# Attention in a fused block: the band masks move from TensorE to VectorE's reduction, key 0 and query 0 move into the bands

## The chip, the cores and the metric

One Trainium2 chip; the kernel runs on one of its NeuronCores. The metric is device time in microseconds (us), the median of several runs. The data path is float32 throughout. Where a product must be exact to float32, both operands are split into a high part (float32r) and a low part, and three products are summed.

## The reference

The program is one transformer layer over x of shape 8 x 512 x 256: layer norm, attention with a mask, residual, layer norm, a mixture of experts, residual. The changed part is the attention:

```python
Q, K, V = (split_heads(xn @ W + b) for W, b in ((Wq, bq), (Wk, bk), (Wv, bv)))    # 16 heads of 16
window_ok = abs(i - j) <= 64
global_ok = (i == 0) | (j == 0)              # query 0 sees all keys, all queries see key 0
scores = einsum('bhqd,bhkd->bhqk', Q, K) * 0.25 + where(window_ok | global_ok, 0, -inf)
out = einsum('bhqk,bhkd->bhqd', softmax(scores), V)
```

After it, each of 16 experts takes its 512 best tokens, computes (gelu(x Wg) * (x Wu)) Wd and adds the weighted rows to the output; 1024 inner columns, 256 outer ones. A shared expert runs for all tokens.

## The kernel before

The program has four blocks, one after another, with a barrier between them: `project` (layer norm, q, k and v), `attend`, `front` (output projection, norm, gate, shared expert, choice of tokens) and `experts`. Each engine has its own stream of instructions in a fixed order written by hand; they meet only at semaphores.

`project` works batch by batch. TensorE makes q and k (four tiles of 128 rows x 512 tokens); ScalarE writes the high parts (line 248), VectorE the low parts (line 299); SP writes all four to the scratch tensor `qk_parts` with one DMA a batch (line 201) from one of two buffers. GpSimd only clears buffers and casts the mask.

`attend` works in steps. One step is one batch and four heads (HQ = 4), so there are 8 x 4 = 32 steps. For each of a step's heads, the keys and queries are cut into four tiles of 128. Tile 0 holds the global key and the global query and is computed against all 512 columns; each other tile only against its window of 256 or 192 columns.

- Scores (`score_job`, lines 633 to 653). Queries on the partitions. They serve only to find each query's maximum. TensorE first writes the mask into PSUM as a bfloat16 product with the identity (line 646), adds the product q k (line 648), and, for tiles 1 to 3, makes a product with keys 0 and 1 alone (line 651). VectorE reduces a group of two or four heads at a time (line 550), the far columns of query 0 apart (line 552), and takes in key 0 (line 555).
- The negated maximum, split in two parts (lines 559 and 561), is transposed by VectorE (line 567) and carried by four small DMAs (`m_rows`, line 495) into rows 96 and 97 of `qs`. There it joins the contraction, so that the second product comes out with the maximum already subtracted.
- Exponents (`st_job`, lines 655 to 675). Keys on the partitions. TensorE makes k q minus the maximum (lines 668 and 670; only tile 0 has a mask product, line 667), and a product with queries 0 and 1 for tiles 1 to 3 (line 673). ScalarE takes the exponential into `pt` (line 610), and that of query 0 into `pq` (line 602). GpSimd zeroes what lies outside the window with two affine selections a tile (line 454).
- Value products (`times_v`, lines 677 to 702), in plain float32, four heads side by side on the array: the window (line 691), the rest of key 0's row (line 697), query 0's column (line 700). One extra column of ones gives the denominators. ScalarE empties the bank (line 595), SP stores it (line 499).

TensorE's order in step u (`body`, line 705) is: for g from 0 to 4, the scores of group g of step u + 2, two exponent jobs of step u, and, from g = 1 on, the value products of tile g - 1 of step u - 1. Scores have two PSUM buffers (of two banks), exponents two of one bank. The loops over batches are hardware loops with the first and last batch peeled.

SP's queue in step u: the four DMAs of `m_rows(u + 1)`; then it waits until TensorE has finished the exponent products of step u and issues the six loads of step u + 4 (line 485), each of 16 partitions x 4 heads x 512 tokens; then the store of step u - 1. Once a batch it also fetches the denominators (`load_den`) and, at t = 3, writes their reciprocals back and waits until they have landed (`store_rden`, line 509 and the wait behind it). VectorE makes those reciprocals after the maxima of step u + 1.

`experts` runs 16 experts. TensorE makes 8 row tiles of h (line 1913); VectorE, ScalarE and GpSimd turn them into high and low parts, GpSimd's low part being the last (line 1803). Then come four output tiles of 128 tokens, each 8 chunks x 3 products (line 1931), in two alternating PSUM banks, which ScalarE empties (line 1849). Output tile 0 waits chunk by chunk for the low parts.

Of the kernel before, what the change touches and what calls it, by code (L numbers as in the profile page):

```python
# [29 lines left out]
P = 128  # L30
# [20 lines left out]
M_ROW = 96  # L51

# [4 lines left out]
W = [h - l for l, h in zip(LO, HI)]  # L57

# [18 lines left out]
def build(nc, d):  # L77

    with ExitStack() as ctx:
# [6 lines left out]
        d["qk"] = scratch("qk_parts", (B, 4, D, S))  # L86
# [12 lines left out]
        ks = att.enter_context(nc.sbuf_tensor("ks", [P, UB, HQ, S], F32R))  # L99
        qs = att.enter_context(nc.sbuf_tensor("qs", [P, UB, HQ, S], F32R))  # L100
        v = att.enter_context(nc.sbuf_tensor("v", [P, B * NT, D], F32))

        mask = att.enter_context(nc.sbuf_tensor("mask16", [P, S + 2 * P], BF16))
# [32 lines left out]
def project(nc, d, sem, tally, ident, bias, eps, ks, qs, vs, mask, ident16):  # L136
    with ExitStack() as ctx:
# [15 lines left out]
        qk = sb("qk", [P, 2, 4, KD, S], F32R)  # L153
        m32 = sb("mask32", [P, S + 2 * P])
# [21 lines left out]
        qlo_s = sem("p_qlo")  # L176
        v_s = sem("p_v")
# [3 lines left out]
        with nc.Block() as block:  # L181
            @block.sync
            def _(sp):
# [45 lines left out]

            @block.scalar  # L230
            def _(act):
# [10 lines left out]
                def qk_hi(b, h, first):  # L242
                    for n in range(4):
# [4 lines left out]
                        act.activation(qk[:, h, 2 * w, m], ps_qk[:, n], ACT.Identity,  # L248
# [23 lines left out]
            def _(dve):  # L272
# [22 lines left out]
                def qk_lo(b, h):  # L295
                    for n in range(4):
                        w, m = n // 2, n % 2
                        dve.wait_ge(qhi_s, b * 4 + (n + 1))
                        dve.scalar_tensor_tensor(out=qk[:, h, 2 * w + 1, m], in0=ps_qk[:, n],
                                                 scalar=bias[:, w, m:m + 1], in1=qk[:, h, 2 * w, m].bitcast(F32),  # L300
# [88 lines left out]
def attend(nc, d, sem, tally, ks, qs, vs, mask, ident16):  # L389
    with ExitStack() as ctx:  # L390
# [3 lines left out]
        SL = UB  # L394
        vx = sb("vx", [P, 2, NT, HQ * VW])
        mx = sb("mx", [P, 2, HQ, NT])
        far = sb("far", [1, HQ])
        nm = sb("nm", [P, 2, HQ * NT], F32R)
        mt = sb("mt", [P, 2, 32])
        pt = [sb(f"pt{i}", [P, 2, HQ, W[i]]) for i in range(NT)]  # L400
        pq = sb("pq", [P, 2, HQ, NT - 1])
# [3 lines left out]
        ps_s = ctx.enter_context(nc.psum_tensor("ps_s", [P, 2, 2 * S], F32))  # L405
        ps_p = ctx.enter_context(nc.psum_tensor("ps_p", [P, 2, S], F32))

        ps_x = ctx.enter_context(nc.psum_tensor("ps_x", [P, 2, HQ, NT - 1, 2], F32))
        key0, query0 = ps_x[:, 0], ps_x[:, 1]  # L410
        ps_o = ctx.enter_context(nc.psum_tensor("ps_o", [P, S], F32))
        qk_in = [sem(f"a_qk_in{s}") for s in range(SL)]
        ones_s = sem("a_ones")
        v_s = sem("a_v")
        m_in = [sem(f"a_m_in{s}") for s in range(SL)]
        sc_s = sem("a_sc")
        mx_s = sem("a_mx")
        mk_s = sem("a_mk")
# [4 lines left out]
        q0_s = sem("a_q0")  # L423
        av_s = sem("a_av")
        sel_s = sem("a_sel")
        nrm_s = sem("a_nrm")
# [6 lines left out]
        GROUPS = [(0, h, 2) for h in range(0, HQ, 2)] + [(j, 0, HQ) for j in range(1, NT)]  # L433
        TJOBS = [(0, h, 1) for h in range(HQ)] + [(i, h, 2) for i in range(1, NT) for h in range(0, HQ, 2)]
        GJ, SJ = len(GROUPS), len(TJOBS)
        EOF = [sum(j[0] < i for j in TJOBS) for i in range(NT + 1)]
        N0 = P + WIN
        MK = P // 32

        def after(b, t, n):

            return b + (t + n) // UB, (t + n) % UB

        with nc.Block() as block:
            @block.gpsimd
            def _(pool):
                def window(b, t, i):

                    wait_alone(pool, tally, exp_s, b * (UB * SJ) + (t * SJ + EOF[i + 1]))
                    for lo, hi, sign in ((0, P, 1), (P, W[i], -1)):
                        part = pt[i][:, t % 2, :, lo:hi]
                        last = pool.affine_select(out=part, in_=part, pattern=[[0, HQ], [sign, hi - lo]],  # L454
                                                  compare_op=ALU.is_ge, fill=0.0, base=0, channel_multiplier=-sign)
                    last.then_inc(sel_s, 1)

                def take_v(b, t, fresh):
                    if not fresh:
                        wait_alone(pool, tally, av_s, b * UB + (t - 1))  # L460
                    src = vs[:, bass.ds(b * NT, NT), t * HQ * DH:(t + 1) * HQ * DH].rearrange("p n (h c) -> p n h c", c=DH)
                    dst = vx[:, t % 2].rearrange("p n (h c) -> p n h c", c=VW)[:, :, :, 0:DH]
                    pool.tensor_copy(dst, src).then_inc(v_s, 1)
# [3 lines left out]
                for t in range(UB):  # L467
                    take_v(0, t, t < 2)
                    for i in range(1, NT):
                        window(0, t, i)  # L470
                with pool.Fori(1, B) as b:
                    for t in range(UB):
                        take_v(b, t, False)
                        for i in range(1, NT):
                            window(b, t, i)

            @block.sync
            def _(sp):
                def load(b, t):

                    def heads(part):
                        return d["qk"][b, part, t * HQ * DH:(t + 1) * HQ * DH, :].rearrange("(h c) q -> c h q", c=DH)

                    for row, part, dst in QK_ROWS:
                        sp.dma_start(dst[row:row + DH, t].bitcast(F32), heads(part)).then_inc(qk_in[t], 16)
# [1515 lines left out]
```

## Time and profile before

| | us |
|---|---|
| median of 3 runs | 1401.46 (1398.49 to 1401.52) |
| the profiled execution | 1400.23 |
| its span | 1398.5 |
| TensorE matmul busy | 1256.7 (90%) |
| VectorE busy | 849.4 (61%) |
| ScalarE busy | 597.1 (43%) |
| GpSimd busy | 584.9 (42%) |
| `attend`: first score, last value product | 119.7, 515.8 |
| `experts`: one expert, start to start | 36.3 |

The span runs from the first to the last recorded instruction; the execution's own time is 1.7 us longer. The page's granted TensorE clock is 0.9 or more in most of its 40 slices, among them all slices of the expert block from 840 us on, and lower where one block hands over to the next. In a timeline, one row can stand for several like instructions (x8); the duration of a matmul is that from its start to its modelled end, and consecutive matmuls overlap, so what a matmul costs is read from start to start, which the prediction calls its pitch. The same holds for VectorE, where a following instruction starts before the end of the one ahead.

### The profile page before, as it was taken

How to read it: one execution, taken by the hardware profiler on the slowest of the kernel's cores; microseconds unless marked ns; L12 is line 12 of the kernel's file. 1: busy time of each engine (PE TensorE's matmuls, PEld its weight loads, DVE VectorE, ACT ScalarE, POOL GpSimd, SP SyncE). 2: the span in 40 equal slices, each digit the busy share in tenths (PEclk: the TensorE clock that was granted, in tenths of full speed). 3: DMA queues.
4: the chain of work that ended last, by engine and by line, in shares of the span. 5: the costliest groups of instructions: out<-in, count | busy, mean ns of one | idle time of the engine just before them, and what ended most of it. 6: DMA issues, size and time to landing. Idle time of an engine off the chain costs nothing. (4 is left out here: it accounts for less than half of the span.)

```text
span 1398.5 us, 26404 instructions
## 1 busy us (share of the span) xinstructions
PE 1256.7 (90%) x9930; PEld 1066.7 (76%) x9930; DVE 849.4 (61%) x1510; ACT 597.1 (43%) x1023; POOL 584.9 (42%) x530
## 2 busy tenths in 40 slices
PE   2995999999999972699999599999999999999997
PEld 2884777777777752588887578888888888888886
DVE  7874555555555512695688676666666666666641
ACT  1340544444444442354222255455455454545442
POOL 6000333332333342462200146666666666665554
PEclk9996999999999985699999789999999999999999
DMA  2778555555555416441003144434444433344411
GB/s 84 262 249 136 79 88 90 86 86 92 93 93 93 71 50 198 144 149 57 15 31 121 51 161 121 115 105 113 120 121 121 121 111 105 109 114 121 121 31 15
DMA packets 71284, 148.44 MB, mean 106 GB/s; under 512 B 14736, under 2 KB 31520, under 8 KB 64928
## 3 DMA queue, kind: packets, MB, share of 16 engines
q1 hardware_dynamic: 58544, 128.39, 35.4%
q0 software_dynamic: 12656, 18.90, 7.4%
q8 instruction: 56, 0.92, 0.3%
q14 instruction: 28, 0.23, 0.1%
HBM read 104.53 MB, written 42.21 MB: 105 GB/s over the span
## 5 line engine op out<-in xcount | busy, mean ns | idle before, releaser
L610 ACT ACTIVATE pt<-ps_p 128x512 f32<-128x512 f32 (+1 forms) x320 | 170.0, 582 | 218.1 <-PE ps_x L673 122.7
L550 DVE TENSOR_REDUCE mx<-ps_s 128x2 f32<-128x384 f32 (+2 forms) x160 | 143.9, 900 | 171.9 <-PE ps_x L651 154.9
L1803 POOL TENSOR_TENSOR h_lo<-h,h_hi 128x512 fp32r<-128x512 f32 x128 | 175.5, 1383 | 136.1 <-ACT h_hi L1839 135.8
L454 POOL TENSOR_SCALAR_AFFINE_SELECT pt<-pt 128x512 f32<-128x512 f32 x192 | 110.1, 597 | 273.4 <-ACT pt L610 273.4
L1913 PE MATMUL ps_gu<-xt_hi,w_hi 128*128 128x512 f32 x512 | 203.5, 397 | 2.1 <-DVE xt_lo L1862 2.1
L1913 PE MATMUL ps_gu<-xt_lo,w_hi 128*128 128x512 f32 x512 | 200.8, 392 | 0.0
L1913 PE MATMUL ps_gu<-xt_hi,w_lo 128*128 128x512 f32 x512 | 200.3, 391 | 0.0
L1878 DVE TENSOR_TENSOR h<-ge,ps_gu 128x512 f32<-128x512 f32 x128 | 87.8, 686 | 180.1 <-ACT ge L1833 167.9
L1740 DVE TENSOR_TENSOR w_lo<-w,w_hi 128x768 fp32r<-128x768 f32 x128 | 173.5, 1360 | 31.3 <-ACT w_hi L1735 27.8
L648 PE MATMUL ps_s<-ks,qs 96*128 96x256 f32 (+2 forms) x512 | 171.6, 398 | 0.0
L1812 POOL DMA_INDIRECT out<-ys,idx x64 | 131.1, 2049 | 73.3 <-ACT ys L1849 61.8
L1931 PE MATMUL ps_y<-w_hi,h_hi 128*128 128x256 f32 x512 | 146.4, 286 | 14.6 <-POOL h_lo L1803 14.6
L646 PE MATMUL ps_s<-mask,ident 128*128 128x256 bf16 (+1 forms) x512 | 139.4, 276 | 16.9 <-DMA ks<-qk_parts 15.9
L1931 PE MATMUL ps_y<-w_lo,h_hi 128*128 128x256 f32 x512 | 144.8, 283 | 0.0
L1931 PE MATMUL ps_y<-w_hi,h_lo 128*128 128x256 f32 x512 | 144.7, 283 | 0.0
L1833 ACT ACTIVATE ge<-ps_gu 128x512 f32<-128x512 f32 x128 | 76.2, 596 | 123.1 <-PE ps_gu L1913 122.4
L1707 POOL DMA_INDIRECT xg<-h_rows,idx x64 | 63.5, 992 | 126.8 <-DVE idx L1698 107.0
L1735 ACT ACTIVATE w_hi<-w 128x768 fp32r<-128x768 f32 x128 | 106.4, 837 | 16.7 <-PEq L880 16.7
L1913 PEld LDWEIGHTS ps_gu<-xt_hi,w_hi 128*128 128x128 f32 x512 | 96.9, 189 | 21.5 <-issue 2.5
L1913 PEld LDWEIGHTS ps_gu<-xt_hi,w_lo 128*128 128x128 f32 x512 | 96.8, 189 | 20.6
L1931 PEld LDWEIGHTS ps_y<-w_hi,h_hi 128*128 128x128 f32 x512 | 98.0, 191 | 18.5 <-POOL h_lo L1803 17.8
L1913 PEld LDWEIGHTS ps_gu<-xt_lo,w_hi 128*128 128x128 f32 x512 | 97.0, 189 | 18.6
(221 smaller groups left out, 2891.9 us busy)
## 6 DMA issues: line engine op xcount, KB each, us to landing
w<-in_We SPq DMA_DIRECT2D x48, 1024.0 KB, 4.9
qk_parts<-qk SPq DMA_DIRECT2D x8, 2048.0 KB, 7.7
qs<-qk_parts SPq DMA_DIRECT2D x96, 128.0 KB, 3.6
ks<-qk_parts SPq DMA_DIRECT2D x96, 128.0 KB, 5.0
x<-in_x SPq DMA_DIRECT2D x16, 512.0 KB, 8.7
attn_t<-on SPq DMA_DIRECT2D x32, 256.0 KB, 3.7
ot<-attn_t SPq DMA_DIRECT2D x32, 128.0 KB
rd<-rden SPq DMA_DIRECT2D x16, 256.0 KB
```

What stands on the lines that cost most here:

```text
L454: last = pool.affine_select(out=part, in_=part, pattern=[[0, HQ], [sign, hi - lo]], compare_op=ALU.is_ge, fill=0.0, base=0, channel_multip ...
L550: last = dve.tensor_reduce(mxu[:, h:h + n, j], tile[:, :, 0:N0 if j == 0 else W[j]], AX, ALU.max)
L610: act.activation(pt[i][:, t % 2, h:h + nh], ps_p[:, n % 2].rearrange("p (h q) -> p h q", h=nh)[:, :, 0:W[i]], ACT.Exp, scale=SCALE).then_i ...
L646: pe.matmul(tile[:, 0:masked], ident16[:], mask[:, m_off:m_off + masked], start=True, stop=False, skip_group_check=True)
L648: last = pe.matmul(tile[:, 0:W[j]], q, ks[0:M_ROW, t, h, LO[j]:HI[j]], start=False, stop=True, skip_group_check=True)
L1735: act.activation(self.hi[:, s, cs], self.w32[:, cs], ACT.Copy).then_inc(self.hi_s, 1)
L1740: eng.tensor_tensor(self.lo[:, s, cs], self.w32[:, cs], self.hi[:, s, cs].bitcast(F32), ALU.subtract).then_inc(self.lo_s, 1)
L1803: pool.tensor_tensor(h_lo[:, m], h32[:, (e * KI + m) % HB], h_hi[:, m].bitcast(F32), ALU.subtract).then_inc(hlo_s, 1)
L1812: pool.indirect_dma_start(d["out"], bass.IndirectOffsetOnAxis(ap=idx[:, e % SLOTS, c:c + 1], axis=0), ys[:, e % 2, c], None, compute_op=AL ...
L1878: dve.tensor_tensor(h32[:, (e * KI + m) % HB], ge[:, m % 2], ps_gu[:, m % 2, 1], ALU.mult).then_inc(h_s, 1)
L1913: last = pe.matmul(ps_gu[:, m % 2, n], l, r, start=c == 0, stop=c == 3 * KD - 1)
L1931: last = pe.matmul(ps_y[:, t % 2, 0:D], l, r, start=c == 0, stop=c == 3 * KI - 1)
```

## The change

Layout. In `qk_parts`, `ks` and `qs` each tile of 128 tokens gets a 129th column (ZC = 129), which holds a copy of token 0: key 0 in `ks`, query 0 in `qs`. A window that starts or passes there therefore contains the global key or query, and is two columns wider (WZ = 258, 258, 194). GpSimd writes the copies in `project`, after the low parts and before the write. The rows of Wq and Wk are permuted on the way in, so that one load reads one run of 4 x 516 floats for each of its 16 partitions.

```diff
-                    sp.wait_ge(qlo_s, b * 4 + 4)
-                    sp.dma_start(d["qk"][b].rearrange("c (m p) q -> p c m q", p=P),
-                                 qk[:, h].bitcast(F32)).then_inc(out_s[h], 16)
+                    sp.wait_ge(z_s, b + 1)
+                    sp.dma_start(d["qk"][b].rearrange("c (m t) d h q -> (t d h) c m q", m=KD),
+                                 qk[:, h].rearrange("p c m k i -> p c m (k i)").bitcast(F32)).then_inc(out_s[h], 16)
...
+                for b in range(B):
+                    pool.wait_ge(qlo_s, b * 4 + 4)
+                    rows = qk[:, b % 2].rearrange("p c m k i -> p (c m) k i")
+                    pool.tensor_copy(rows[:, :, :, P], rows[:, :, 0, 0:1].to_broadcast([P, 4 * KD, NT])).then_inc(z_s, 1)
```

Scores. One product a head and tile, without a mask, in a ring of three banks. VectorE adds the mask (bfloat16, in SBUF) and takes the maximum in one instruction, 16 a step.

```diff
+                    if n >= RING:
+                        pe.wait_ge(mx_s, n + 1 - RING)
+                    q = tile_of(qs[0:M_ROW, t, h], j)
+                    k = ks[0:M_ROW, t, h]
+                    k = whole(k) if j == 0 else window(k, j)
+                    out = ps_s[:, n % RING]
+                    out = out.rearrange("p (k c) -> p k c", c=P) if j == 0 else out[:, 0:WZ[j]]
+                    pe.matmul(out, q, k, start=True, stop=True).then_inc(sc_s, 1)
...
+                        n, m = (S, mask[:, 0:S]) if j == 0 else (WZ[j], mask[:, S:S + WZ[j]])
+                        dve.tensor_tensor_reduce(junk[:, (u * SG + g) % RING, 0:n], ps_s[:, (u * SG + g) % RING, 0:n], m, 1.0, -3e38, ALU.add, ALU.max,
+                                                 mx[:, u % 2, h, j:j + 1]).then_inc(mx_s, 1)
```

Exponents. Two heads a job throughout, in two buffers of two banks; the product with query 0 alone and `pq` go, since query 0 is a column of the band (`FAR`). Before the products of a step ScalarE copies the two maximum rows of query 0 to the added columns (`far_rows`), and TensorE waits for that. GpSimd masks pieces of 64 columns (`near_only`: 4, 4 and 3 selections a step in place of two a tile).

TensorE's order. Each of eight places of a step has two scores of step u + 2 and one exponent job of step u; the value products of step u - 1 stand at two places.

```diff
+                for u in range(NU):
+                    for n in range(SJ):
+                        if u + 2 < NU:
+                            score(u + 2, 2 * n)
+                            score(u + 2, 2 * n + 1)
+                        exponents(u, n)
+                        if u >= 1 and n in (5, 7):
+                            times_v(u - 1, n - 5)
+                            times_v(u - 1, n - 4)
```

SP's queue and the reciprocals. The loops of `attend` are unrolled on all engines.

```diff
+                for u in range(NU):
+                    b, t = u // UB, u % UB
+                    if u + 1 < NU:
+                        m_rows(u + 1)
+                    if 1 <= u <= NU - UB:
+                        sp.wait_ge(st_s, u * SJ)
+                        load(u + UB - 1)
+                    if u >= 2:
+                        store(u - 2)
+                    if b >= 1 and t == 2:
                         load_den(b - 1)
+                    if b >= 1 and t == 3:
                         store_rden(b - 1)
...
+                for u in range(NU):
+                    maxima(u)
+                    if u >= 9 and u % UB == 1:
+                        reciprocals((u - 9) // UB)
                 reciprocals(B - 2)
```

Experts. Chunks 0 to 6 of output tiles 0 and 1 go ahead of chunk 7 of both:

```diff
+                    if e > 0:
+                        pe.wait_ge(ys_s, e * CT)
+                    contract(0, range(KI - 1))
+                    contract(1, range(KI - 1))
+                    contract(0, range(KI - 1, KI)).then_inc(y_s, 1)
+                    contract(1, range(KI - 1, KI)).then_inc(y_s, 1)
+                    for t in range(2, CT):
+                        pe.wait_ge(ys_s, e * CT + (t - 1))
+                        contract(t, range(KI)).then_inc(y_s, 1)
```

## Rows read from the trace of the kernel before

**Rows 1.** Windows, one step: engines' busy us (instructions), granted clock, DMA share, GB/s.
```profile
core 0: us, PE busy (x) PEld busy (x) DVE busy (x) ACT busy (x) POOL busy (x), PEclk, DMA share, GB/s
253.10:265.20 12.10, 12.07 (x142) 9.38 (x142) 6.66 (x12) 5.73 (x13) 3.83 (x8) 1.00 0.52 91
```
**Rows 2.** Timeline of TensorE in a step: start us, duration us, engine, line, operation.
```profile
250.18 0.28 PE L646 MATMUL ps_s<-mask,ident 128*128 128x256 bf16 x1
...
250.46 0.36 PE L670 MATMUL ps_p<-qs,ks 128*128 128x256 f32 x1
...
251.44 0.64 PE L691 MATMUL ps_o<-pt,vx 128*32 128x256 f32 x8
...
252.04 0.36 PE L670 MATMUL ps_p<-qs,ks 128*128 128x192 f32 x1
...
254.59 0.26 PE L646 MATMUL ps_s<-mask,ident 128*128 128x192 bf16 x1
...
254.94 0.26 PE L646 MATMUL ps_s<-mask,ident 128*128 128x192 bf16 x1
...
257.66 0.53 PE L691 MATMUL ps_o<-pt,vx 128*32 128x192 f32 x8
...
258.80 0.28 PE L646 MATMUL ps_s<-mask,ident 128*128 128x256 bf16 x1
```
**Rows 3.** Timeline of an expert's contraction; in brackets idle time and releaser.
```profile
1018.70 0.28 PE L1931 MATMUL ps_y<-w_hi,h_lo 128*128 128x256 f32 x1
...
1019.89 0.39 PE L1931 MATMUL ps_y<-w_hi,h_hi 128*128 128x256 f32 x1 [0.91 <-POOL h_lo L1803]
...
1020.55 0.47 ACT L1849 ACTIVATE ys<-ps_y,wt 128x256 f32<-128x256 f32 x1 [0.35 <-PE ps_y L1931]
```
**Rows 4.** Timeline of TensorE, products of 512 and 256 columns without a mask.
```profile
683.99 0.39 PE L1456 MATMUL ps_gu<-ht_b,sw_lo 128*128 128x512 f32 x1
684.22 0.28 PE L1491 MATMUL ps_y<-sw_hi,h_hi 128*128 128x256 f32 x1
684.34 0.28 PE L1491 MATMUL ps_y<-sw_lo,h_hi 128*128 128x256 f32 x1
```
**Rows 5.** Timeline of VectorE, an operation with an accumulator.
```profile
684.65 0.75 DVE L1205 TENSOR_SCALAR_CACHE_REDUCE junk<-seg_probs,cand 128x512 bf16<-128x512 f32 x1
685.32 0.08 DVE L1205 DVE_READ_ACCUMULATOR junk<-seg_probs,cand 128x1 f32 x1
685.32 0.68 DVE L1158 TENSOR_TENSOR h<-ge,ps_gu 128x512 f32<-128x512 f32 x1
```
**Rows 6.** Timeline of VectorE, a scan and a plain two-input operation.
```profile
760.52 1.23 DVE L1242 TENSOR_TENSOR_SCAN run<-equal,zero 128x512 f32<-128x512 f32 x1
...
789.91 0.42 DVE L1168 TENSOR_TENSOR x<-ps_y,x 128x256 f32<-128x256 f32 x1
790.25 1.21 DVE L1682 TENSOR_TENSOR hot<-pm,iota 128x1024 bf16<-128x1024 bf16 x1
```
**Rows 7.** Timeline of VectorE, the end of a step's maxima.
```profile
255.46 0.17 DVE L559 TENSOR_SCALAR nm<-mx 128x16 fp32r<-128x16 f32 x1
...
256.07 0.56 DVE L550 TENSOR_REDUCE mx<-ps_s 128x2 f32<-128x384 f32 x1
```
**Rows 8.** Timeline of SP's queue: loads, the reciprocals' write, maximum rows.
```profile
277.60 1.30 SPq L485 DMA_DIRECT2D qs<-qk_parts  x3
...
282.69 0.36 SPq L509 DMA_DIRECT2D rden<-den  x1
286.51 2.62 SPq L495 DMA_DIRECT2D qs<-mt  x4
```
**Rows 9.** One line, 277 to 281 us: duration ns min/median/max, first and last start.
```profile
L485 SPq DMA_DIRECT2D ks<-qk_parts x3: 316/316/369, 279.1 to 280.0; - x3
...
DMA to landing us min/median/max: 3.0/4.4/5.4
```
**Rows 10.** Windows: the last write of q and k; the queued first loads.
```profile
106.00:109.00 3.00, 0.00 (x0) 0.00 (x0) 0.00 (x0) 0.00 (x0) 0.00 (x0) 0.80 1.05 367
122.00:125.00 3.00, 2.96 (x17) 2.46 (x16) 2.13 (x4) 0.00 (x0) 0.00 (x0) 0.50 1.09 131
```

More of the change, by code:

```diff
@@ L51 @@
 M_ROW = 96
+RING = 3
+ZC = P + 1
+ZS = NT * ZC
 LO = [0] + [P * i - WIN for i in range(1, NT)]
@@ L430, in attend, with whole, window, tile_of @@
         rden_out = sem("a_rden_out")
[L433 to L436, printed above, removed]
+        SCORES = [(j, h) for j in range(NT) for h in range(HQ)]
+        TJOBS = [(i, p) for i in range(NT) for p in range(HQ // 2)]
+        SG, SJ = len(SCORES), len(TJOBS)
         N0 = P + WIN
         MK = P // 32
-        def after(b, t, n):
-            return b + (t + n) // UB, (t + n) % UB
+        LOADS, MROWS = 6, MK
+        def whole(tile):
+            return tile.rearrange("p (k c) -> p k c", c=ZC)[:, :, 0:P]
+        def window(tile, n):
+            return tile[:, ZC * n - WIN - 1:ZC * n - WIN - 1 + WZ[n]]
+        def tile_of(tile, n):
+            return tile[:, ZC * n:ZC * n + P]
         with nc.Block() as block:
@@ L466, in _ @@
                 pool.wait_ge(ones_s, 1)
-                for t in range(UB):
-                    take_v(0, t, t < 2)
+                for u in range(NU):
+                    take_v(u)
                     for i in range(1, NT):
[L470 to L475, printed above, removed]
+                        near_only(u, i)
@@ L477, in _ @@
             @block.sync
             def _(sp):
[L479 to L485, printed above, removed]
-                QK_ROWS = [(DH * r, part, dst) for dst, parts in ((qs, (0, 0, 1)), (ks, (2, 3, 2)))
-                           for r, part in enumerate(parts)]
@@ L655, in st_job @@
[L655 to L665 removed]
+                        pe.wait_ge(qk_in[t], (b + 1) * 16 * LOADS)
@@ L675, in st_job, with near @@
                     last.then_inc(st_s, 1)
-                def times_v(b, t, i, first):
+                def near(rows, v, p, i):
+                    out = ps_o[rows, LO[i]:HI[i]]
+                    if i < NT - 1:
+                        pe.matmul(out.rearrange("p (k c) -> p k c", c=WIN), v,
+                                  p.rearrange("p (k c) -> p k c", c=WIN + 1)[:, :, 0:WIN],
+                                  start=False, stop=True, skip_group_check=True)
+                    else:
+                        pe.matmul(out[:, 0:WIN], v, p[:, 0:WIN], start=False, stop=True, skip_group_check=True)
+                        pe.matmul(out[:, WIN:W[i]], v, p[:, WIN + 1:W[i] + 1], start=False, stop=True, skip_group_check=True)
@@ L693, in times_v @@
                     for h in range(HQ):
-                        rows = slice(32 * h, 32 * h + 32)
-                        v = vx[:, t % 2, i, h * VW:(h + 1) * VW]
+                        rows, v = slice(32 * h, 32 * h + 32), vx[:, s, i, h * VW:(h + 1) * VW]
                         if i == 0:
-                            last = pe.matmul(ps_o[rows, N0:S], v[0:1], pt[0][0:1, t % 2, h, N0:S], start=False, stop=True,
+                            last = pe.matmul(ps_o[rows, N0:S], v[0:1], pt[0][0:1, s, h, N0:S], start=False, stop=True,
@@ L698, in times_v @@
                                              skip_group_check=True)
                         else:
-                            last = pe.matmul(ps_o[rows, 0:1], v, pq[:, t % 2, h, i - 1:i], start=False, stop=True,
+                            z = FAR[i]
+                            last = pe.matmul(ps_o[rows, 0:1], v, pt[i][:, s, h, z:z + 1], start=False, stop=True,
                                              skip_group_check=True)
```

354 lines of the change are left out of this document (149 added, 205 removed).

## The prediction

> **What bounds the kernel now.** I read the windows of single attention steps first, because the change touches the attention block, one wait of the projection block and one loop of the expert block. A step (one batch, four of 16 heads; 32 in all) takes 12.1 us; TensorE is busy for 12.07 of them at granted clock 1.00, VectorE for 6.66, ScalarE for 5.73, GpSimd for 3.83 [rows 1]. TensorE never stops, the others stand for half of the time, so its stream is the step. Then I took its timeline apart by start to start [rows 2]: a mask, a windowed score and a two-column key-0 product are 250.18 to 250.46, 0.28 us for one head; a mask and a 512-column product 0.35 us (254.59 to 254.94); the value products of a 256-wide key tile 0.60 us (251.44 to 252.04), those of tile 0 1.14 us (257.66 to 258.80). The expert block I read by its one regular hole: each expert's TensorE stops before the last contraction chunk, 1018.70 to 1019.89 [rows 3], against a pitch of 0.12 us (684.22 to 684.34) [rows 4], so for 1.07 us.
>
> **TensorE's step afterwards.** Masks and two-column products leave the scores: 4 of 512 columns, 8 of 258, 4 of 194. A 512-column float32r product alone has pitch 0.23 us (683.99 to 684.22), a 256-column one 0.12 [rows 4]; 258 I put at 0.125, and 194 at 0.12 too (bounds 0.08, in proportion to its columns, and 0.12: a window of 192 in the present step is no cheaper than one of 256). Scores: 0.92 + 1.0 + 0.48 = 2.4 us. Exponent products: 4 x 0.35 for tile 0 with its mask, 12 x 0.12 without their partners = 2.8. Value products keep their work; the 64-wide pieces split one matmul of tile 3 in two (4 more a step) and the query-0 column is read from the band: 1.14 + 0.60 + 0.60 + 0.55 = 2.9. The sum is 8.1 us instead of 12.1. If TensorE stayed the bound that would be 4 us x 32 = 128 us. It does not.
>
> **VectorE's step afterwards.** Instead of 5 reductions, 2 far reductions and 2 small maxima it runs 16 add-and-maximum instructions, 4 over 512 elements, 8 over 258, 4 over 194, each with an accumulator. The trace has none. Nearest rows: a 512-element operation with accumulator goes from 684.65 to the next full instruction at 685.32, 0.67 us, the accumulator read (0.08) lying beside its successor [rows 5]; a plain two-input operation of 256 has pitch 0.34 (789.91 to 790.25) [rows 6]. I take 0.67, 0.40 and 0.34: 2.68 + 3.2 + 1.35 = 7.2 us. Bounds: 0.61, 0.34, 0.27 (6.2 us in all), and the 1.23 us of the scan over 512, half the rate [rows 6], with 0.67 and 0.53 for the shorter ones (about 0.13 plus two cycles' share an element): 12.4 us. I take the accumulator row as the nearest kind. The tail (two small operations and the transpose) is 255.46 to 256.07, 0.61 us [rows 7], and about 0.25 for the last reduction's end: 0.85.
> The Trainium skill ("VectorE: DVE Perf Modes", Rules for kernel authors) says to minimise the number of VectorE operations, since each pays its drain; this speaks against 16 operations in place of 9. By the pitch rows each of the 16 carries about 0.13 us that no element pays for, and that is in my sum.
>
> **How the two interlock.** TensorE's scores run three banks ahead at most (RING = 3). After score 11 it makes one exponent job and the value products of tiles 0 and 1: 0.13 + 0.24 + 1.14 + 0.60 us, and 0.4 until score 12 can be read: 2.5 us, while VectorE holds at most three reductions less what has run, 1.1 us. It idles 1.4 us. After score 15 the hole is 2.0 us against 1.0 us of reductions and 0.85 of tail: idle 0.3 with the wake-ups. VectorE's cycle is 7.2 + 0.85 + 1.4 + 0.3 = 9.8 us; TensorE waits for it. ScalarE has the same exponentials in fewer instructions (5.7 us now), GpSimd 11 selections instead of 6, at most 0.6 us each by its 3.83 us for 7 instructions [rows 1], 7 us: both hide below 9.8. The copy of far rows takes the place of the query-0 exponentials.
>
> **SP's queue, which moves.** Per step it issues four row DMAs (286.51, 2.62 us), then six loads; the first is issued at 277.60 [rows 8] and the sixth at 280.0, landing 5.4 us later [rows 9], 7.8 us in all. The rows of step u+1 wait for its maxima, the loads stand behind them, and they bring what the scores of step u+3, run at the start of step u+1, need. Before, loads started 1.3 us before a step and had the whole 12.1 us. Now the chain is 2.6 + 0.4 + 7.8 = 10.8 us from the end of the maxima. Over two steps: scores and maxima of a step about 9.6 us (9.8 less their late start), then 10.8: 20.4, or 10.2 a step, hardly above VectorE's 9.8 and partly taken up; I take 10.1. The rows of a load are now one run of 8256 bytes instead of four of 2048. Bounds for the load burst: 4.9 us (issue and the earliest landing of 3.0) to 8.5; I take no gain: the queued loads at the start, 2048-byte runs into 16 partitions, move 131 GB/s at full DMA share, the write of q and k, also in 2048-byte runs but over 128 partitions, 367 [rows 10]. So the narrow target holds them, not the run length, and it stays.
> The Trainium skill ("SBUF — State Buffer", Door 1: The DMA port swizzle) states that 16 partitions reach only 4 of the 16 ports and measures 104 GB/s there. The trace agrees in kind, its 131 GB/s being for loads that overlap on two such ranges.
> **The wait inside the queue.** store_rden waits on SP until its DMA has landed: from 282.69 to the next issue at 286.51, 3.8 us [rows 8]. Before, the loads had slack. Now SP reaches it in step 4b+3, and the reciprocal (0.54 us) stands behind maxima(4b+5), the very maxima whose rows are queued next. Those rows, the loads and the scores behind them are 0.54 + 3.8 = 4.4 us late. It hits 6 times (u = 7 to 27; at 31 no load follows): 26 us.
> **Attention in sum:** 30 steps x (12.1 - 10.1) = 60, less 26 = 34 us. The first body is some 3 us shorter, the last two, without scores, about as much longer behind ScalarE and GpSimd: nought. The start is DMA and VectorE as now. Unrolled loops: priced at nothing (bounds -2 to +5), the expert block being straight code already.
>
> **Projection.** GpSimd's 32-element copy (about 0.4 us) goes between the last low part and the write of q and k. Batches hide it behind the other half's buffer; after the last batch the barrier feels it: +0.4 us (0 to 2, should rows of 2064 bytes write worse).
>
> **Experts.** Chunks 0 to 6 of tiles 0 and 1 now go before chunk 7: 21 more matmuls, 2.5 us, cover the 1.07. But tile 2 needs bank 0 emptied: 0.28 to the end of its last matmul, 0.05, 0.47 us for the copy (1020.55) [rows 3] and 0.05 to wake, against 0.36 us of chunk 7 of tile 1: a new stop of 0.45. Net 0.6 x 16 = 10 us (bounds 0 and 17).
>
> **Sum:** the profiled execution took 1400.2 us (span 1398.5), within 0.1% of the median 1401.46. 1400.2 - 34 - 10 + 0.4 = 1357 us.
>
> **Rivals.**
> (B) The load chain never binds: longer runs land sooner. For it: a quarter of the descriptors, and writes in the rows may be slower than reads for another reason than the target. Then 9.8 us a step and between none and half of the 26 us: 1400 - 69 - 10 = 1321, or 1337.
> (C) The new operation carries 0.1 us more overhead: 16 x 0.1, of which 1.3 a step shows: about 1395, little or no gain. For it: it is an operation that the trace doesn't have; against: the accumulator row.
> (D) Slower: the add-and-maximum runs at two cycles an element, like the scan [rows 6]. VectorE then needs 12.4 + 0.85 + about 1 = 14.2 us: 32 x 2.1 - 10 = 57 us more, 1458. It decides from 0.17 us above my price per instruction. 
> (E) The clock: TensorE, now waiting a fifth of each step and 4 us at six places, is granted 0.50. In the first stretch of attention it stood at 0.50 (1.2 GHz) although TensorE was busy for 2.96 of 3.00 us [rows 10]. At half the clock a step of 8.1 us comes to some 15: about 1490. Against: the expert block keeps 0.9 or more in every slice of the page in spite of its stops.
>
> **Chances:** forecast 0.42 (own range 1340 to 1377), B 0.20, C 0.20, D 0.10, E 0.08. 1322 to 1397 leaves out D, E and a little of B and C. What a measurement tells from no change is 0.3%, 4 us. Faster by more: 0.42 + 0.20 + 0.15 = 0.77; within: 0.05 of C; slower 0.18.
>
> **What would show it.** In the trace after: VectorE near 8 us busy in a step of 10, and TensorE near 80%, waiting for the maxima; pitches of 0.67, 0.40 and 0.34; one step in four near 14.5 us, with TensorE waiting for the DMA of ks and SP standing behind rden; in the experts a stop of 0.45 us in place of 1.07, behind the copy of ps_y. Steps under 9.6 us, or no long fourth step, would prove the queue argument wrong; pitches above 0.8 us my choice among the rows.

## The result, and the profile after

The changed kernel takes 1357.22 us (median of 4 runs, 1356.25 to 1364.43); the kernel before, beside it on the same chip, 1401.49 (4 runs, 1398.49 to 1406.84). The ratio is 0.969, 95% interval 0.965 to 0.974, and the prediction was 1357. The profiled execution took 1356.66 us, span 1354.9. What the spans lost, 1398.5 - 1354.9 = 43.6 us, I cut at three events of TensorE in both timelines: the last value product of attention starts at 515.8 before and 487.8 after (28.0 us less); from there to the first product of expert 0 it is 292.4 and 288.9 us (3.5 less, in code that the change doesn't touch); the experts follow from the line below.

Instructions of one line (TensorE, first product of the experts): duration ns min/median/max, first to last start. First the kernel before, then the one after.
```profile
L1913 PE MATMUL ps_gu<-xt_hi,w_hi x512: 389/389/767, 808.2 to 1376.8; 128*128 128x512 f32 x171
```
```profile
L1885 PE MATMUL ps_gu<-xt_hi,w_hi x512: 389/389/764, 776.7 to 1333.9; 128*128 128x512 f32 x171
```
568.6 against 557.2 us: 11.4 less, and 0.7 in the end that is left.

The step. These windows answer to [rows 1]: an undisturbed step, and the next, which waits for loads.
```profile
core 0: us, PE busy (x) PEld busy (x) DVE busy (x) ACT busy (x) POOL busy (x), PEclk, DMA share, GB/s
253.95:263.71 9.76, 9.71 (x109) 6.40 (x109) 7.25 (x36) 5.83 (x10) 3.35 (x9) 1.00 0.71 111
263.71:277.21 13.50, 9.76 (x118) 6.41 (x108) 7.50 (x36) 5.82 (x10) 5.60 (x16) 1.00 0.54 90
```
By the starts of the first score of each step, the 29 steps from 133.88 to 453.06 us are: 10.7 and 12.9 at the start (10.7 the first body, without value products), then 21 ordinary ones, mostly in a pattern of 10.6, 10.8 and 9.8 (mean 10.45), and a long one at u = 8, 12, 16, 20, 24 and 28: 12.5, 13.5, 12.4, 12.6, 12.7, 12.6. The places are the predicted ones; the lengths are not (10.1 and 14.5). In the first body TensorE makes two scores and then stands for ScalarE's copy of the far rows:
```profile
137.03 0.50 PE L637 MATMUL ps_p<-mask,ident 128*128 128x192 bf16 x2 [1.96 <-ACT qs L586]
```

VectorE's timeline, which answers to [rows 5] and [rows 6]: start us, duration us, operation.
```profile
250.83 0.36 DVE L548 CUSTOM_DVE_ANT_0 junk_s<-ps_s,mask 128x194 bf16<-128x194 f32 x1 [1.71 <-PE ps_s L625]
251.12 0.08 DVE L548 DVE_READ_ACCUMULATOR2_ANT mx<- 128x1 f32 x1
251.12 0.35 DVE L548 CUSTOM_DVE_ANT_0 junk_s<-ps_s,mask 128x194 bf16<-128x194 f32 x1
251.40 0.08 DVE L548 DVE_READ_ACCUMULATOR2_ANT mx<- 128x1 f32 x1
...
255.22 0.69 DVE L548 CUSTOM_DVE_ANT_0 junk_s<-ps_s,mask 128x512 bf16<-128x512 f32 x1
...
255.83 0.69 DVE L548 CUSTOM_DVE_ANT_0 junk_s<-ps_s,mask 128x512 bf16<-128x512 f32 x1
...
257.05 0.42 DVE L548 CUSTOM_DVE_ANT_0 junk_s<-ps_s,mask 128x258 bf16<-128x258 f32 x1
...
257.40 0.42 DVE L548 CUSTOM_DVE_ANT_0 junk_s<-ps_s,mask 128x258 bf16<-128x258 f32 x1
```
The pitches are 0.61 (255.22 to 255.83), 0.35 (257.05 to 257.40) and 0.28 us (251.12 to 251.40), and the accumulator read costs nothing of its own. They sum to 4 x 0.61 + 8 x 0.345 + 4 x 0.28 = 6.3 us.

SP's queue across a long step, answering to [rows 8], then what TensorE does at its end:
```profile
264.08 0.34 SPq L515 DMA_DIRECT2D rden<-den  x1
266.67 2.58 SPq L500 DMA_DIRECT2D qs<-mt  x4
269.31 1.32 SPq L492 DMA_DIRECT2D qs<-qk_parts  x3
270.67 1.58 SPq L492 DMA_DIRECT2D ks<-qk_parts  x3
```
```profile
277.21 0.73 PE L625 MATMUL ps_s<-ks,qs 96*128 96x512 f32 x2 [3.69 <-DMA ks<-qk_parts]
```
SP stands from 264.42 to 266.67 behind the write of the reciprocals, although the maxima of that step were transposed by 263.61 (VectorE's row at 263.40, 0.21 us). Rows and loads go out late, and TensorE stops for 3.69 us. This is the longest of the six: here the write lands 2.6 us after its issue, in four of the others after 1.5. The other five long steps have stops of 2.61 to 2.86 us, and the second step has one of 2.70.

Waits between 110 and 490 us (engine and line, what it waited for: us, times, longest):
```profile
PE ps_s L625 <- DMA ks<-qk_parts: 43.6, 17, 15.9
PEld ps_s L625 <- DVE mx L548: 34.6, 159, 0.9
PEld ps_o L653 <- POOL pt L467: 15.6, 30, 0.5
```
15.9 us of the first row is the start of attention, which the kernel before has too; the other 27.7 us are the steps' own.

### The profile page after: what moved, and what is told of

It is laid out like the page before. It is cut to its first block and busy times, and to the rows that moved or that the text cites. A ratio compares the mean times of both kernels' runs of the same rounds, so it can differ in the third digit from the quotient of the medians.

```text
span 1354.9 us, 23514 instructions
## 1 busy us (share of the span) xinstructions
PE 1191.9 (88%) x8906; PEld 979.6 (72%) x8906; DVE 868.0 (64%) x2246; ACT 599.0 (44%) x959; POOL 612.8 (45%) x698
## 5 line engine op out<-in xcount | busy, mean ns | idle before, releaser
L548 DVE CUSTOM_DVE_ANT_0 junk_s<-ps_s,mask 128x258 bf16<-128x258 f32 (+2 forms) x512 | 211.9, 472 | 123.5 <-PE ps_s L625 122.1
L601 ACT ACTIVATE pt<-ps_p 128x516 f32<-128x516 f32 (+2 forms) x256 | 167.7, 682 | 158.3 <-PE ps_p L643 94.5
L467 POOL TENSOR_SCALAR_AFFINE_SELECT pt<-pt 128x256 f32<-128x256 f32 x352 | 132.3, 415 | 230.3 <-ACT pt L601 230.3
L1775 POOL TENSOR_TENSOR h_lo<-h,h_hi 128x512 fp32r<-128x512 f32 x128 | 178.8, 1408 | 119.6 <-ACT h_hi L1811 119.3
L625 PE MATMUL ps_s<-ks,qs 96*128 96x258 f32 (+2 forms) x512 | 164.6, 380 | 45.6 <-DMA ks<-qk_parts 43.6
L1784 POOL DMA_INDIRECT out<-ys,idx x64 | 137.1, 2142 | 72.3 <-ACT ys L1821 57.4
L625 PEld LDWEIGHTS ps_s<-ks,qs 96*128 96x128 f32 x512 | 99.3, 207 | 87.1 <-DMA ks<-qk_parts 45.2
```

The source lines that it names most:

```text
L548: dve.tensor_tensor_reduce(junk[:, (u * SG + g) % RING, 0:n], ps_s[:, (u * SG + g) % RING, 0:n], m, 1.0, -3e38, ALU.add, ALU.max, mx[:, u ...
L601: act.activation(dst, src, ACT.Exp, scale=SCALE).then_inc(exp_s, 1)
L625: pe.matmul(out, q, k, start=True, stop=True).then_inc(sc_s, 1)
L1775: pool.tensor_tensor(h_lo[:, m], h32[:, (e * KI + m) % HB], h_hi[:, m].bitcast(F32), ALU.subtract).then_inc(hlo_s, 1)
L1784: pool.indirect_dma_start(d["out"], bass.IndirectOffsetOnAxis(ap=idx[:, e % SLOTS, c:c + 1], axis=0), ys[:, e % 2, c], None, compute_op=AL ...
```

## Experiments

Each time stands beside runs of the kernel before on the same chip (medians 1401 to 1402 us), and the ratios are to those.

**e1: the expert contraction in its old order** (the loop below in place of `contract`).
```diff
+    for t in range(CT):
+        if e > 0 or t >= 2:
+            pe.wait_ge(ys_s, e * CT + (t - 1))
+        for k in range(KI):
...
```

> The changed kernel with the experts' contraction in its old order. If the new order is worth what the traces show (an expert takes 35.60 us instead of 36.30, 16 of them), this runs in 1357 + 11 = 1368 us, and the attention part alone is the other 33 us. Rival: the hole in the contraction was slack that comes back elsewhere; then 1357 to 1360.

1373.06 us (1372.17 to 1376.85), ratio 0.979 (0.974 to 0.985): 15.8 us above the changed kernel. Its traced execution was its slowest, and the two spans are 20.2 us apart. The experts take 784.4 to 1353.4 = 569.0 us there, 11.8 of the 20.2. Another 7.4 lie in untouched code ahead of the experts, at another granted clock, and 0.6 behind the last start. Windows of that stretch, first here, then in the changed kernel:
```profile
640.00:650.00 10.00, 10.00 (x58) 9.66 (x59) 1.75 (x4) 2.51 (x3) 1.26 (x1) 0.69 0.00 0
650.00:660.00 10.00, 8.67 (x37) 7.20 (x37) 5.29 (x16) 3.74 (x5) 2.72 (x3) 0.80 0.15 52
```
```profile
640.00:650.00 10.00, 9.98 (x67) 8.65 (x66) 5.15 (x10) 4.43 (x5) 1.27 (x1) 1.00 0.15 52
650.00:660.00 10.00, 8.89 (x51) 7.62 (x52) 7.81 (x27) 2.46 (x4) 5.85 (x5) 1.00 0.01 2
```

**e8, the other side: the kernel before with the new contraction alone** (`contract` put into it, nothing else).

> The kernel before with the new order of the expert contraction alone. It is the other side of e1_old_contraction, which came out 16 us slower than the changed kernel. If the reorder is worth what the period of an expert says (36.30 to 35.60 us, 16 times): 1401.5 - 11 = 1390. If it is worth the 16 us of the pair after and e1: 1385. If it needs the rest of the change: 1395 to 1401.

1389.58 us (1387.14 to 1394.78), ratio 0.991 (0.988 to 0.994). The experts run from 809.5 to 1366.7, 557.2 us, the figure of the changed kernel. So the reorder is worth 11.4 to 11.8 us on either side. TensorE's stops in the contraction over all 16 experts, in the kernel before and in the changed one:
```profile
PE ps_y L1931 <- POOL h_lo L1803: 14.6, 16, 0.9
```
```profile
PE ps_y L1902 <- ACT ys L1821: 3.4, 16, 0.2
```
0.2 us an expert is left, where 0.45 was predicted; e8 has the same 3.4 us in 16 stops.

**e2: the reciprocals' write one step later, its landing waited for only ahead of the next read.**
```diff
-                    sp.wait_ge(rden_out, b * 16 + 16)
...
+                    if b >= 2 and t == 0:
+                        store_rden(b - 2)
                     if b >= 1 and t == 2:
+                        if b >= 2:
+                            sp.wait_ge(rden_out, (b - 1) * 16)
                         load_den(b - 1)
-                    if b >= 1 and t == 3:
-                        store_rden(b - 1)
```

> The changed kernel, but SP issues the write of the reciprocals at the end of the next step's queue, when they are long ready, and waits for its landing only two steps later, before den is loaded again. Queue theory: the six long steps (12.7 us against 10.5) go, and the stretch at granted clock 0.50 behind each of them: 13 to 20 us, so 1337 to 1344. Rival (the loads themselves are late every fourth step, whatever SP waits for, because the fetch of the denominators is in front of them): no change, 1354 to 1358.

1342.5 us (1340.45 to 1343.59), ratio 0.958 (0.952 to 0.963): 14.7 less. The long steps are gone (9.7 to 10.8 from u = 7 on). SP's queue at the place shown above:
```profile
264.19 1.34 SPq L492 DMA_DIRECT2D ks<-qk_parts  x3
265.56 0.43 SPq L504 DMA_DIRECT2D attn_t<-on  x1
266.04 0.43 SPq L515 DMA_DIRECT2D rden<-den  x1
270.60 2.61 SPq L500 DMA_DIRECT2D qs<-mt  x4
```
The wait inside the queue is shown as the cause of the long steps from u = 8 on. The second step stays at 12.8. TensorE still stops for ks at the start of most steps, for up to 0.9 us.

**e3: no loads of q and k after the first four steps.**
```diff
-                        load(u + UB - 1)
+                        pass
...
-                        pe.wait_ge(qk_in[t], (b + 1) * 16 * LOADS)
+                        pe.wait_ge(qk_in[t], 16 * LOADS)
```

> The changed kernel without the loads of q and k after the first four steps (later steps compute on the first batch's data). Queue theory: every step becomes 9.7 to 9.8 us, as the one step in four that waits for no DMA already is; 28 steps x 1.1 = 30 us, so 1327. Rival (VectorE and TensorE alone make the steps what they are): 1350 or more.

1323.17 us (2 runs), ratio 0.944 (0.937 to 0.951), every step from the third on 9.73 us. The wait for the reciprocals' landing is still in SP's queue here, so it costs only through the loads behind it. That is near rival B's number, 1321, reached by taking the chain away, not by its being hidden.

**e7: the loads ahead of the row DMAs** (on top of e2; the copy of the far rows moves behind the last exponential).
```diff
-                    if u + 1 < NU:
-                        m_rows(u + 1)
                     if 1 <= u <= NU - UB:
                         sp.wait_ge(st_s, u * SJ)
                         load(u + UB - 1)
...
+                    if u + 1 < NU:
+                        m_rows(u + 1)
...
-                        if n == 5 and u + 1 < NU:
+                        if n == 7 and u + 1 < NU:
                             far_rows(u + 1)
```

> As e2_rden_later, but in SP's queue the six loads of a step stand ahead of its four row DMAs, and ScalarE copies the far rows after its last exponential instead of after the sixth. Theory (the chain maxima, row DMAs 2.6, loads 7.8 us is what makes steps of 10.1 to 10.8 us out of 9.7): the loads start 2.6 us sooner, every step is 9.7 to 10.0, and the time 1342.5 - 29 x 0.4 = 1331 (1326 to 1335). Rival (the row DMAs now stand 2.4 us later and share the queues with the loads, and the exponents of the next step wait for them and for the copy): steps of 10.5 to 12, 1345 to 1390.

1325.27 us (1320.35 to 1326.97), ratio 0.945 (0.942 to 0.948): 17 us below e2, whose interval it doesn't touch, 32 below the changed kernel, with the same work done. From the third on all steps are 9.7 to 9.8 us, and no wait for ks is left among them; the second falls from 12.8 to 10.1, the first body rises from 10.6 to 12.8. SP's queue and one step:
```profile
244.07 1.25 SPq L492 DMA_DIRECT2D qs<-qk_parts  x3
245.37 2.34 SPq L492 DMA_DIRECT2D ks<-qk_parts  x3
247.75 2.67 SPq L500 DMA_DIRECT2D qs<-mt  x4
```
```profile
245.00:254.76 9.76, 9.70 (x119) 6.41 (x109) 7.26 (x36) 5.82 (x10) 4.49 (x13) 1.00 0.67 113
```
The loads start 0.9 us ahead of the step at 245.00; in the changed kernel they stood behind the four rows. The chain maxima, rows, loads is shown as the second half of what separates the changed kernel from 1323. The later copy of the far rows came in the same edit and wasn't tried alone; e3, which leaves it where it was, has the same steps.

The other runs ask what holds the 9.75 us.

**e4: a shorter first key tile** (the maximum of tile 0 over 192 of 512 columns).
```diff
-                        n, m = (S, mask[:, 0:S]) if j == 0 else ...
+                        n, m = (N0, mask[:, 0:N0]) if j == 0 else ...
```

> The changed kernel with tile 0's maximum taken over 192 of its 512 columns (query 0's far keys are left out of its maximum). VectorE does 4 x 0.33 = 1.3 us less a step. If VectorE's work sets the step: 30 x 1.3 = 39 us less, 1318. If the chain maxima, rows, loads sets it over two steps: half of that, 1337. If TensorE's own order with its two blocks of value products does: under 10 us, 1347 or more.

1361.69 us (1360.72 to 1373.18), ratio 0.974 (0.967 to 0.981): no gain, and the steps are the same, 9.7 for the short ones. VectorE's amount of work is not what sets them.

**e5 and e6: ScalarE's copy of the outputs later**, with the loads (on top of e2) and without them (on top of e3).
```diff
-                        if n == 0 and u >= 2:
+                        if n == 3 and u >= 2:
                             out_rows(u - 2)
```

> Attention as changed with two edits on the SP and the ScalarE side: the write of the reciprocals is queued a step later with its landing awaited before the next read (as in e2_rden_later, 1342.5 us), and ScalarE's copy of the outputs (0.59 us) stands after exponential 3 of a step instead of after exponential 0. Theory (the 9.7-us step is held by ScalarE's order at its start: exponential 0, copy, exponential 1 = 2.6 us, for which TensorE's third exponent job waits): steps that the load chain does not hold lose about 0.5 us, the others nothing; 1336 to 1340. Rival (the 9.7 is held by VectorE's maxima or by the value products): 1342, no change. Second rival (the copy now delays exponential 4 or the value products of the following hole): 1345 to 1350.

1338.34 us (1337.61 to 1340.37), ratio 0.954 (0.952 to 0.957). That is 4 us less than e2 by the medians and inside what the theory expected, but the intervals of the two ratios overlap, so a gain isn't shown.

> The changed kernel without the loads of q and k after the first four steps (later steps compute on the q and k of the first batch, so the attention of batches 1 to 7 is left out of the reference), and with ScalarE's copy of the outputs after exponential 3 instead of 0. Beside e3_no_loads (1323.2, every step 9.73 us). Theory (ScalarE's order at the start of a step): steps of 9.2 us, 29 x 0.5 = 15 us less, 1308. Rival (VectorE or the value products hold the step): 9.7 and 1323.

1323.78 us (2 runs), ratio 0.944 (0.940 to 0.947), steps of 9.62 instead of 9.73. My expectation of 9.2 fell: the copy alone holds 0.1 us.

**e9 and e10: value products at four places, a tile each** (on top of e7), and the same with e5's copy.
```diff
-                        if u >= 1 and n in (5, 7):
-                            times_v(u - 1, n - 5)
-                            times_v(u - 1, n - 4)
+                        if u >= 1 and n >= 4:
+                            times_v(u - 1, n - 4)
```

> e7_loads_ahead with the value products of one key tile after each of the last four exponent jobs, instead of two tiles after the sixth and two after the eighth. e7 came out at 1325.3 with every step 9.75 us; in such a step VectorE stands 1.7 us (behind the products of tiles 0 and 1) and 0.7 us (behind tiles 2 and 3), since TensorE runs only three banks ahead. Theory (the 9.75 is VectorE's 6.2 us of reductions, 0.6 us of tail and these two holes): holes of a tile each are mostly covered by the three banks, steps of about 8.9 us, 1325 - 29 x 0.85 = 1300 (1294 to 1308). Rival (ScalarE's order at the start of a step, exponential, copy, exponential, holds it): 9.5 to 9.75, 1318 to 1325. Second rival (the products now wait for GpSimd's selections, which come later): 10 us or more, 1332.

1324.61 us (1322.75 to 1325.16), ratio 0.945 (0.943 to 0.948), steps of 9.6 to 9.8: no gain. VectorE's longest hole shrank from 1.7 to 1.1 us, and the step did not.

> e9_four_places with ScalarE's copy of the outputs after exponential 3 instead of 0. If VectorE's holes alone held the step (theory): no more than 2 us below e9. If the two limits lie on top of one another (the holes and ScalarE's order, each enough for 9.6 to 9.75): both must go, steps of 8.5 us, 1325 - 29 x 1.2 = 1290, while e9 alone brings little.

1353.02 us (1350.02 to 1357.6), ratio 0.966 (0.963 to 0.969). Slower, against both theories: the products of tile 0 now wait for the copy that frees ps_o, in steps of 10.3 to 10.5 where e9 has 9.65. Three steps near the end are longer still, 12.2 to 14.8 us; TensorE's granted clock is 0.50 for half of their time (see the last section). They are 8 to 9 us of the 27 that the steps lose against e9.
```profile
254.65 0.53 PE L676 MATMUL ps_o<-pt,vx 128*32 128x192 f32 x8 [0.58 <-ACT on L582]
```

**e11: short first tile and copy later together** (e4's and e5's edits on top of e7).

> e7_loads_ahead with a first key tile whose maximum is taken over 192 of 512 columns (query 0's far keys are left out of its maximum, so VectorE has 1.3 us less to do a step) and ScalarE's copy after exponential 3. e4_short_first_tile (the first of these edits) and e6_no_loads_copy_later (the second) each left the step at 9.6 to 9.75 us. If the limits lie on top of one another: steps of 8.6 to 9.0 us, 1325 - 29 x 0.9 = 1299. If a third thing holds 9.6 (the value products of TensorE's two places and the selections before them): 9.6, 1321 to 1325.

1320.33 us (1314.59 to 1323.9), ratio 0.942 (0.938 to 0.946), steps of 9.55: the pair doesn't lift it either. This run has the step with the least waiting, and by it TensorE's own stream can be counted (start us, duration us):
```profile
230.75 0.73 PE L628 MATMUL ps_s<-ks,qs 96*128 96x512 f32 x2
...
233.15 0.41 PE L628 MATMUL ps_s<-ks,qs 96*128 96x258 f32 x2
233.40 0.40 PE L649 MATMUL ps_p<-qs,ks 128*128 128x258 f32 x2
233.64 0.71 PE L628 MATMUL ps_s<-ks,qs 96*128 96x258 f32 x2
...
236.21 0.53 PE L676 MATMUL ps_o<-pt,vx 128*32 128x192 f32 x8
...
237.94 0.47 PE L628 MATMUL ps_s<-ks,qs 96*128 96x194 f32 x2
...
238.47 0.65 PE L628 MATMUL ps_s<-ks,qs 96*128 96x194 f32 x2
...
239.27 0.64 PE L656 MATMUL ps_o<-pt,vx 128*32 128x256 f32 x8
...
240.31 0.51 PE L628 MATMUL ps_s<-ks,qs 96*128 96x512 f32 x1
```
A round of two 258-wide scores and their exponent job takes 0.49 us undisturbed (233.15 to 233.64). The first two rounds take 2.40 us, the four with 258 columns 4 x 0.49 = 1.96 of the 3.06 that pass until 236.21, the value products 1.73 and 1.04, the two rounds between them 2 x 0.53 of 1.33: 8.2 us of work, close to the predicted 8.1, and 1.37 of waiting, though the view shows TensorE busy nearly throughout. Where it waits, by the waits of that kernel from 150 to 420 us (28 steps): on the maxima, GpSimd's selections and the exponentials, together 1.5 us a step.
```profile
PEld ps_s L628 <- DVE mx L551: 19.2, 84, 0.3
...
PEld ps_o L656 <- POOL pt L467: 15.0, 29, 0.5
...
PEld ps_p L649 <- ACT pt L604: 7.8, 28, 0.3
```

**e12: value products spread over the whole step** (on top of e7).
```diff
-                        if u >= 1 and n in (5, 7):
...
+                        if u >= 1 and n in (1, 3, 5, 6):
+                            times_v(u - 1, (1, 3, 5, 6).index(n))
...
-                        if n == 0 and u >= 2:
-                            out_rows(u - 2)
...
+                        if n == 7 and u >= 1:
+                            out_rows(u - 1)
```

> e7_loads_ahead (1325.3 us, every step 9.75) with the value products of the step before spread over the step: tile 0 after exponent job 1, tile 1 after 3, tile 2 after 5, tile 3 after 6, and ScalarE's copy of those outputs after its last exponential, where it stands still. Of the earlier tries each engine's busy time fitted below 9.6 (VectorE 6.9, ScalarE 5.8, TensorE's own stream 8.2 to 8.4), and none of the single removals moved the step. Theory (the step is uneven: in its first half VectorE's 512-wide maxima and ScalarE's 0.9-us exponentials come faster than they are worked off, in its second half both stand while TensorE makes value products, and 3 and 2 banks don't bridge that): with the products spread, TensorE's stream alone is the bound, steps of 8.5 to 8.9 us, 1325 - 29 x 1.05 = 1295 (1288 to 1302). Rival (TensorE's stream is really 9.6 us, as it is shown busy throughout): 9.6 and 1320 to 1325. Second rival (the loads, whose slots are now freed no earlier, hold a shorter step): 9.2 and 1309.

1327.81 us (1325.57 to 1335.36), ratio 0.948 (0.945 to 0.950), steps of 9.9 to 10.3. The theory fell. TensorE now also waits at the start of a step for the copy of the far rows (0.20 us with a bracket, 0.41 from start to start beyond the two scores), and behind each block of value products its scores stop again for the maxima:
```profile
PEld ps_s L627 <- DVE mx L551: 41.1, 135, 0.6
PEld ps_p L639 <- ACT qs L589: 13.8, 27, 0.5
```
(150 to 420 us; in e7 the first is 33.8 us in 166 waits.)

## Why the prediction came out right

**TensorE's step and "it does not stay the bound": right.** 12.07 us busy of 12.1 became 8.2 us of work (as counted in e11) in a step of 9.6 to 9.8 without the chain.

**VectorE's pitches: each too high.** 0.67, 0.40 and 0.34 were taken; 0.61, 0.345 and 0.28 were measured, the lower bounds. The nearest row by kind (an operation with an accumulator, two SBUF operands in and out) was not the nearest in cost. Rivals C and D fall with it. The Trainium skill ("Vector Engine (DVE) Microarchitecture Reference", Points that are easy to get wrong) names half rate where both sources are non-bf16 ones in SBUF, which isn't the case here. The trace agrees: 0.61 us for 512 elements, half of the scan's 1.23.

**"VectorE's cycle 9.8, TensorE waits for it": the number held, its reason not.** Reductions came to 6.3 us instead of 7.2, the holes behind the value products to 1.7 and 0.75 instead of 1.4 and 0.3, and with the 0.85 of the tail that is again 9.6. But with 1.3 us less to do (e4) VectorE just stood longer: from 150 to 420 us it waited 117 us for scores, 88 in the changed kernel. In e11, with no load in the way, the same cut left 9.55 of 9.75. So VectorE's amount of work, which the forecast summed, isn't the bound. What is, is not shown. TensorE, VectorE and ScalarE hand work through rings of three and two banks, and with TensorE's blocks of value products at each of the places tried there were waits on one side or the other. Five variants (e4, e6, e9, e11, e12) left a step of 9.55 to 10.3 us. Which change would shorten it stays open.

**The chain through SP: right, and a little short.** Ordinary steps were put at 10.1 and came at 10.45. Over 27 steps, the six long ones on the same base, that is 9 us lost; the second step, 12.9, lost another 2.8. In part the burst of six loads was longer than the 7.8 us taken: from first issue to last landing 8.1 us (median from 150 to 430 us; 7.7 before), which makes 9.6 + 3.0 + 8.1 = 20.7, or 10.35 a step. The loads did not land sooner for their longer runs, as predicted. Landing of all loads from 150 to 430 us, before and after:
```profile
DMA to landing us min/median/max: 2.7/4.2/5.6
```
```profile
DMA to landing us min/median/max: 3.0/4.9/6.3
```
The Trainium skill ("SBUF — State Buffer", Door 1: The DMA port swizzle) has a 16-partition target reach 4 of the 16 ports. That the loads gained nothing agrees with it, but no run here changed the run length or the number of partitions alone.

**The wait inside the queue: right in place, too dear.** Predicted 4.4 us at six places, 26 in all; measured 2.3 above an ordinary step (12.71 - 10.45), 14 in all, and e2 gives back 14.7. The term that was off is the landing of the reciprocals' write, put at [rows 8]'s 3.8 us from its issue to the next: that is 1.5 us in four of the six places, 1.8 in one and 2.6 in the one shown above. The write now lands 1.4 to 2.6 us after its issue (3.2 to 3.5 before). From the end of the transpose to the first row's issue it comes to 2.2 us on average, where 4.4 was taken. The 12 to 13 us gained so are about what the other steps lost.
```profile
L515 SPq DMA_DIRECT2D rden<-den x7: 344/345/432, 219.7 to 478.7; - x7
...
DMA to landing us min/median/max: 1.4/1.5/2.6
```

**Attention in sum: 34 predicted, 28 measured.** The 28 steps behind the first body took 338.2 us before and take 308.5: 29.7 less. The forecast for 28 steps is 28 x 2.0 - 26.4 = 29.6, nearly the same number, by errors of opposite sign: the two paragraphs above. The shortfall lies at the ends. The forecast had two more steps' gain, 4 us, and nought for the rest. Measured, the first body starts 3.0 us earlier (133.88 against 136.88), takes 1.4 us more instead of some 3 less (10.7 against 9.3; the wait for the far rows, which the forecast priced at nothing, is 1.96, and the mean granted clock of this body is 0.65), and what follows the last start is 3.1 us longer (34.7 against 31.6), at granted clock 0.82 where the kernel before had 1.00.

**Projection: nothing lost.** Its last write is issued at 102.67 us (102.56 before) and the first load of attention at 110.31 (110.39); 0.4 had been allowed.

**Experts: 10 predicted, 11.4 measured**, since the new stop is 0.2 us and not 0.45.

**The untouched block, 3.5 us: not in the sum.** It took 289 to 292 us in the two kernels, and from 286.2 (e10) to 297.5 (e12) in all 14 traces; e1's is 7.4 us above the changed kernel's, at another clock. So the 3.5 are no more than it varies by itself. With the experts it made up for attention's shortfall, so the hit within 0.3 us is luck on top of a sound estimate: -28 - 11.4 - 3.5 - 0.7 stands where -34 - 10 + 0.4 was written. Rival B's premise failed, its price of a step without the chain held. Rival E came true only in small: see the last section.

**Slips in the recorded sums.** None moves the 1357. Rival B's second figure is 1321 + 13 = 1334, not 1337. The lower bound of a load burst is 2.4 + 3.0 = 5.4 us by [rows 9], not 4.9. Rival D's threshold comes to (12.1 - 0.85 - 1 - 7.2) / 16 = 0.19 us an instruction by its own terms, not 0.17. Rival E's "every slice" isn't so: the expert block's first slice on the page, 804 to 839 us, shows 0.8; only from 840 us on are all at 0.9 or more.

## What to carry to other kernels

When an edit shortens a step, recount each queue's chain against the new step: waits and issue order that had 12 us were harmless, at 10 us one queue's wait and one pair in the wrong order were 32 of the 34 us between the changed kernel and the same kernel without its loads. Where engines hand work through short rings, busy times below the step don't say which one binds; take work away from one and see whether it merely waits longer. Check a hit term by term: here terms wrong by some 12 us each way cancelled. Price a new instruction by both nearest rows, and leave untouched code a few microseconds for the clock.

## What the runs showed of the hardware

The changed kernel has seven stops of 2.6 to 3.7 us behind the first body, and with each of them TensorE's granted clock falls to 0.50 (1.2 GHz) for 3 us or more. In five cases it falls 0.6 to 1.8 us after TensorE resumed, though TensorE was then busy throughout; in two (before 408.42 and 453.06) about 1 us ahead of that. The seven stops of 0.9 to 1.1 us between them left it at 1.00. Windows behind the stop shown above, to 282 us:
```profile
277.21:278.00 0.79, 0.79 (x5) 0.51 (x5) 0.14 (x1) 0.00 (x0) 0.00 (x0) 0.90 1.14 251
278.00:279.00 1.00, 1.00 (x5) 0.81 (x4) 1.00 (x3) 0.00 (x0) 0.00 (x0) 0.50 1.00 140
...
280.00:281.00 1.00, 1.00 (x5) 0.89 (x4) 0.96 (x4) 0.73 (x2) 0.00 (x0) 0.50 1.04 116
281.00:282.00 1.00, 0.95 (x7) 0.66 (x5) 0.51 (x3) 0.68 (x1) 0.00 (x0) 0.87 1.01 132
```
In e2 the stops between 220 and 420 us are at most 0.9 us long, and the clock is 1.00 throughout that stretch:
```profile
220.00:420.00 200.00, 190.17 (x2077) 124.98 (x2077) 141.94 (x686) 113.90 (x195) 85.25 (x229) 1.00 0.68 108
```
A long stop is not the only thing that comes ahead of 0.50. In e10 the clock falls at 380.5 us and again at 394.2, for 10 us each time, though TensorE had not stopped for over 0.6 us at once from 163 to 380 us; what brought it down there is open. The slow stretch costs little behind a stop: the step after the one at 277.21 is 11.0 us, the one after 408.42 11.6, against 10.45.

The add-and-maximum with an accumulator ran at 0.61 us for 512 elements with one operand in PSUM and a bfloat16 one in SBUF: less than the 0.67 of the accumulator row in [rows 5]. Its accumulator read lies beside the next instruction, as in that row.
